# Attention with row sums on GpSimd: the last add of a group becomes a fifth adding transfer, and three orders of issue move

## What is computed

```python
attn = jnp.einsum('bhqd,bhkd->bhqk', q, k) * scale      # 16 heads of 32
attn = jax.nn.softmax(attn, axis=-1)
out = jnp.einsum('bhqk,bhkd->bhqd', attn, v)
```

## Time and profile before

| | |
|---|---|
| median of three runs | 4841.78 us (4838.85 to 4843.54) |
| the profiled execution's own time | 4836.55 us |
| its span, first to last instruction | 4834.7 us |
| PE busy | 4691.4 us, 97% of the span |
| POOL busy | 3223.0 us, 67% |
| DVE busy | 3170.4 us, 66% |
| ACT busy | 2398.9 us, 50% |
| adding transfers (L840) | 256, 1024 KB each, median 7.3 us from issue to landing |

### The profile page before, as it was taken

One profiled execution on the slowest core, in us unless ns is written; L12 is line 12 of the kernel. 1 busy time (PEld: TensorE's weight loads), 2 busy tenths in 40 slices (PEclk: granted clock), 3 DMA queues, 4 the chain that ended last, 5 costly groups with the idle time before them and its releaser, 6 DMA issues. The chain is left out here.

```text
span 4834.7 us, 66456 instructions
## 1 busy us (share of the span) xinstructions
PE 4691.4 (97%) x24396; PEld 2773.0 (57%) x24396; DVE 3170.4 (66%) x5296; ACT 2398.9 (50%) x4653; POOL 3223.0 (67%) x1117
## 2 busy tenths in 40 slices
PE   8999999999899999999999999999999999999979
PEld 6887878878654444444444444444444444444447
DVE  4223232333188888888888888888888888888534
ACT  2111121121146666666666666666666666666621
POOL 1121212121249998989989989999899998998920
PEclk9999999999979999999999999999999999999989
DMA  5344343343346655656656566665665656655466
GB/s 172 103 127 122 109 138 102 119 129 111 91 106 130 137 127 125 138 125 137 133 124 139 124 131 136 126 139 120 132 137 124 140 125 132 137 124 121 90 225 236
DMA packets 254215, 633.49 MB, mean 131 GB/s; under 512 B 45252, under 2 KB 79044, under 8 KB 212936
## 3 DMA queue, kind: packets, MB, share of 16 engines
q0 software_dynamic: 36864, 268.45, 27.8%
q1 hardware_dynamic: 217032, 360.85, 27.0%
HBM read 224.96 MB, written 134.74 MB: 74 GB/s over the span
## 5 line engine op out<-in xcount | busy, mean ns | idle before, releaser
L927 DVE TENSOR_REDUCE unit_max<-mx_ps 128x1 f32<-128x512 f32 x4096 | 2535.2, 681 | 317.0 <-PE mx_ps L1002 310.9
L836 POOL TENSOR_TENSOR p_pair<-p_sb 128x2048 f32<-128x2048 f32 x512 | 2439.8, 4811 | 185.3 <-PE mx_ps L1026 128.3
L913 ACT ACTIVATE p_sb<-st_ps 128x512 f32<-128x512 f32 x4096 | 2061.9, 628 | 905.5 <-PE st_ps L1073 905.5
L1002 PE MATMUL mx_ps<-k_x,q_x 96*128 96x512 f32 x4096 | 1684.9, 415 | 21.5 <-DMA k_x<-k_lo_d 19.6
L1073 PE MATMUL st_ps<-q_x,k_x 97*128 97x512 f32 x4096 | 1607.8, 413 | 37.9 <-ACT p_sb L913 37.3
L1073 PEld LDWEIGHTS st_ps<-q_x,k_x 97*128 97x128 f32 x4096 | 770.3, 188 | 599.3 <-ACT p_sb L913 512.8
L1002 PEld LDWEIGHTS mx_ps<-k_x,q_x 96*128 96x128 f32 x4096 | 784.6, 192 | 456.7 <-DVE unit_max L927 234.3
L1014 PE MATMUL o_ps<-p_sb,v_sb 128*32 128x512 f32 x8192 | 986.8, 599 | 0.0
L285 POOL TENSOR_TENSOR h_lo<-h_f,h_hi 128x512 fp32r<-128x512 f32 x128 | 165.2, 1291 | 687.7 <-DVE h_hi L469 687.7
L1014 PEld LDWEIGHTS o_ps<-p_sb,v_sb 128*32 128x32 f32 x8192 | 214.0, 109 | 494.1 <-ACT p_sb L913 309.8
L469 DVE CAST h_hi<-h_f 128x512 fp32r<-128x512 f32 x128 | 55.0, 431 | 541.9 <-ACT h_f L342 541.9
(11 more groups left out here) (94 smaller groups left out, 3926.8 us busy)
## 6 DMA issues: line engine op xcount, KB each, us to landing
p_pair<-p_pair POOLq DMA_DIRECT2D x256, 1024.0 KB, 7.3
q_x<-q_hi_d SPq DMA_DIRECT2D x128, 256.0 KB, 8.6
k_x<-k_hi_d SPq DMA_DIRECT2D x68, 256.0 KB, 7.3
xt<-x SPq DMA_DIRECT2D x64, 256.0 KB, 2.7
stage<-w SPq DMA_DIRECT2D x32, 512.0 KB, 5.1
q_hi_d<-qk_hi SPq DMA_DIRECT2D x64, 256.0 KB, 3.0
q_lo_d<-qk_lo SPq DMA_DIRECT2D x64, 256.0 KB, 3.9
k_hi_d<-qk_hi SPq DMA_DIRECT2D x64, 256.0 KB, 2.6
```

The costliest lines, as they stand in the source:

```text
L836: pool.tensor_tensor(p_pair[:, slot, :, :], p_sb[:, n % SLOTS, :, :], p_sb[:, (n + 1) % SLOTS, :, :], ALU.add).then_inc(pair_done, 1)
L913: act.activation(p_sb[:, (L * G * KT + n) % SLOTS, h, :], st_ps[bank(g, m)][:, :], ACT.Exp, scale=SCALE).then_inc(exp_done, 1)
L927: dve.reduce_max(unit_max[:, n // 4, n % 4:n % 4 + 1], mx_ps[UNIT_PLACE[n] % RING][:, :], AX.X).then_inc(bank_read, 1)
L1002: pe.matmul(mx_ps[UNIT_PLACE[n] % RING][:, :], q_x[qc][0:R, h, t * P:(t + 1) * P], k_x[u][0:R, h, kc * 512:(kc + 1) * 512], start=True, st ...
```

## The change

The ninth add of a group becomes a fifth `join` (so `NA` is 8 and `NJ` is 5), and the third sum waits for five joins. The next group's pair 0 goes ahead of the wait for it and pair 1 behind. `normalise` moves from behind the fourth join to ahead of pair 6. `spread_inverse` is split, and its store goes ahead of `load_shift`. In the strings, the unit behind the products moves to a later place of the step.

```diff
-    NA, NJ = NP + 1, 4
-    PARTS = [(2, 0, False, 7), (4, 0, True, 10), (0, NA, False, 11)]
+    NA, NJ = NP, 5
+    PARTS = [(2, 0, False, 7), (4, 0, True, 10), (5, 0, False, 11)]
...
-        STEPS = ["USUSUSUVUSSUSUSUS", "USUSUSUVUSSUSUSUS", "USUSUSUVZUSSUSUSUS", "USUSUSUVZUSSUSUSUS",
...
+        STEPS = ["USUSUSUVSSUSUUSUS", "USUSUSUVSSUSUUSUS", "USUSUSUVZSSUSUUSUS", "USUSUSUVZSSUSUUSUS",
...
-                def spread_inverse(count):
-
+                def store_inverse(count):
                     sp.wait_ge(inv_done, count)
                     sp.dma_start(inv_d.rearrange("h (r n) -> (h r) n", n=QR), inv_t[:, :]).then_inc(inv_st, 16)
+
+                def spread_inverse(count):
+
                     sp.wait_ge(inv_st, count * 16)
...
                             spread_sums(read_count(L, g, PART_PLACE[LAST_PART], first, last))
+                        if not (first and g == 0):
+                            store_inverse(L * G + g)
                         if not (last and g == G - 1):
                             load_shift(L * G + g + 2, (qc + 1) % QC)
...
                     if at > 0:
+                        pool.wait_ge(joined, (at * NJ - 1) * 16)
+                    pair(at, 0, a)
+                    if at > 0:
                         pool.wait_ge(joined, at * NJ * 16)
-                    pair(at, 0, a)
-                    pool.wait_ge(pair_done, at * NA)
                     pair(at, 1, b)
...
                     pair(at, 5, c)
+                    if at > 0:
+                        normalise(at)
                     pool.wait_ge(sum_done, at * NS + 1)
                     pair(at, 6, a)
                     pool.wait_ge(pair_done, at * NA + 6)
                     pool.wait_ge(joined, (at * NJ + 3) * 16)
                     join(d, c)
-                    if at > 0:
-                        normalise(at)
                     pair(at, 7, b)
                     pool.wait_ge(pair_done, at * NA + NP)
-                    pool.tensor_tensor(p_pair[:, a, :, :], p_pair[:, a, :, :], p_pair[:, b, :, :], ALU.add).then_inc(pair_done, 1)
+                    pool.wait_ge(joined, (at * NJ + 4) * 16)
+                    join(a, b)
```

More of the change, by code:

```diff
@@ L648, in attention_stage @@
         SK = 4 * KT
-        STEPS = ["USUSUSUVUSSUSUSUS", "USUSUSUVUSSUSUSUS", "USUSUSUVZUSSUSUSUS", "USUSUSUVZUSSUSUSUS",
-                 "USUSUSUVUSSUSUSUS", "USUSUSUVUSSUSUSUS", "USUSUSUVTUSSUSUSUS", "USUSUSUVZUSSUSUSUS"]
+        STEPS = ["USUSUSUVSSUSUUSUS", "USUSUSUVSSUSUUSUS", "USUSUSUVZSSUSUUSUS", "USUSUSUVZSSUSUUSUS",
+                 "USUSUSUVSSUSUUSUS", "USUSUSUVSSUSUUSUS", "USUSUSUVTSSUSUUSUS", "USUSUSUVZSSUSUUSUS"]
         FIRST = sum(s.count("U") for s in STEPS[AHEAD:])
@@ L807, in _ @@
                 spread_sums(ALL_READS + len(PARTS_AT) - PARTS_IN)
+                store_inverse(NQ * QC)
                 spread_inverse(NQ * QC)
```

## The result

The changed kernel takes 5035.9 us in the median of four runs (5024.07 to 5060.09), against 4842.66 us before (four runs as well): 1.0406 times as long, 95% interval 1.0366 to 1.0445. It is 193 us slower. Its profiled execution took 5038.24 us.

What follows compares the result with a forecast made beforehand. PE bounds the kernel now, but POOL's ring, 48.9 + 3.9 = 52.8 us, would set the period: +129 for 60 groups, -7 for the last four, +4 at the end, +126 on 4836.55, forecast 4968 us, range 4775 to 5040.

Steps and rivals of the forecast that it cites:

- POOL's ring: POOL's chain of joins and pairs through one group: 48.9 us base, 52.8 with slower landings, setting the period above PE's.
- The order on SP: Early product puts SP's loads ahead of join 4: lead 3.8 us, or 2.4 at a set's first group.
- named signs: Join 4 landing in 9 to 13 us, others 7.3; each set's first group longest; last four groups about 49.
- extra landing: Join 4's added landing time behind loads: 3.2 us ordinarily, 6.0 in a set's first group, mean 3.9 (3.0 to 5.3).
- the link from join 2 to join 3: Part of POOL's chain, a landing then an issue, with pair 4 hidden in it: 7.82 us.
- Work less lead: Join 4 ends behind the loads' work: for 1.5 MB, 7.0 us of work, lead 3.8, extra 3.2.
- It makes the product's new place possible: Inverses' store ahead of the shift row, load landing near 2534.6; costed at nothing by itself.
- The early product: Product ahead of pair 6, in POOL's 2.3 us wait for PE, ending ACT's wait: -0.87 us a group.
- the order of product and loads: Product ahead of pair 6 lets SP issue loads before join 4, lengthening its landing.
- The strings: PE's steps: three scores start one matmul earlier, ACT 0.23 us earlier; -0.8 us a group at best, 0 at worst.
- Landings that hardly grow: Rival: join 4 keeps 7.3 to 7.5 us, group 49.0 to 49.8, time 4744 to 4790, say 4765; chance 0.22.
- Half the extra: Rival: loads cost a transfer 1.2 to 2.9 us in the mean; 4808 to 4910 us, 4850 at 1.9; chance 0.12.

Runs made afterwards that it cites:

- experiment 8: The changed kernel without the loads for the next heads, so part of the work is left out: 4783.81 us, ratio 0.9878 to the kernel before.
- experiment 1: The changed kernel with the next heads' loads held until the fifth transfer of the group before has landed: 4854.55 us, ratio 1.0023 to the kernel before.
- experiment 7: The changed kernel with the loads held until pair 6 is done, to issue them together with the fourth transfer: 5102.65 us, ratio 1.0535.
- experiment 3: The kernel before with only the fifth transfer in place of the ninth add, the product staying behind the fourth transfer: 5046.16 us, ratio 1.0418.
- experiment 6: The changed kernel with its ninth add back on POOL and the loads held until the fourth transfer has landed: 4758.5 us, ratio 0.983.
- experiment 10: Early product, new strings, ninth add, loads held until the fourth landing, but the inverses' store back behind the shift row: 4883.11 us, ratio 1.0083.
- experiment 11: The kernel before with early product, early store of inverses, and loads held until the fourth transfer has landed: 4799.4 us, ratio 0.9911.
- experiments 5: The kernel before with only the early product and early store of the inverses, ninth add and old strings kept: 4977.46 us, ratio 1.0284.
- experiment 4: The kernel before with the new strings alone: 4813.94 us, ratio 0.9945.
- experiments 2: The changed kernel with its ninth add back on POOL and four transfers: 4944.65 us, ratio 1.0211 to the kernel before.

## Why the prediction was right, and where it was off

**The cause was right.** The forecast was 4968 us for 5035.9, slower. The range, 4775 to 5040, held it by only 4 us, and one of the four runs, at 5060, lies outside: that it held is in part luck. POOL's ring over the landings of the fourth and fifth transfers sets the period. Experiment 8 takes the loads away, and the ring falls to 49.5 us, near the base of 48.9 that the prediction had; experiment 1 moves them and gets 180 us back. The order on SP turned round with a lead of 3.8 us, as worked out from the product's place. At a set's first group it is 2.4 us, as forecast, though the prediction does not show how it gets from 3.5 us behind the last score to that lead. A set's first group is the longest, and the last four, without loads, are 48.9 to 51.2 us apart. Two of the named signs were a little off: at a set's first group join 4 lands in 14.1 us, not in 9 to 13, and join 2 in 7.8 us in the mean, not 7.3.

**The size was off by a third**: +126 us forecast, +193 measured. The mis-sized term is the ring's length, 52.8 us for 53.9, and 60 groups make that single microsecond some 60 us. Half of it is the fourth transfer's extra landing, 4.4 us in the mean (11.7 less 7.3) where I took 3.9: 3.6 for 3.2 in the ordinary groups and 6.8 for 6.0 in a set's first. The other half is the link from join 2 to join 3, 8.31 us for 7.82. I had read it from one group in the earlier trace rows that was on the short side (the mean before was 7.97), and the second transfer, too, now lands later. It does so without loads as well (7.7 us in experiment 8), and why is open. The range's upper end for the extra, 5.3, covered it.

**The rule behind the extra was only partly right.** "Work less lead" holds in experiment 1, where the loads are issued 4.9 us ahead of the first transfer, and 5.2 at a set's first group: it gives 9.4 and 12.6 us, and 9.4 and 12.6 were measured. In the changed kernel it gives 10.5 for 10.8 us at a lead of 3.8, and 15.4 for 14.1 at a set's first group. It fails at no lead (experiment 7), and it fails in experiment 3. There the loads are issued 5.3 us ahead of the fifth transfer, which makes 9.0 us for 1.5 MB, and 12.6 were measured. In the group shown the fourth transfer was on the way until 2731.84, over the first 4.8 us of that lead, so the lead on SP is not the lead in work; no run tests that by itself.

The Trainium skill (DMA: Bandwidth & Descriptors, "Queues, rings and completion order") has each DMA engine take turns between its queues, packet by packet. Even turns would make 12 us the ceiling, by an estimate: 7.3 us and the transfer's own work of 1 MB again, 4.7 us at the rate of the loads. The trace agrees in part: behind 1.5 and 1.75 MB the fourth transfer of the changed kernel keeps to it in the mean (10.8 and 11.2 us), behind 2.25 MB it does not (14.1), and in experiment 7 it keeps to it beside 1.5 MB alone. Whether the packets' unequal sizes or the ordered increment of the same section makes the difference, no run here tells.

**"It makes the product's new place possible", costed at nothing by itself.** With the loads held it is worth 125 us: the early product and the new strings gain 82 us with it (experiment 6) and lose 41 without it (experiment 10). In the changed kernel itself no run puts the store back.

**The early product was costed as a gain of 0.87 us a group.** With the loads held it is one (-43 us, experiment 11). As written it is worth +137 us, because it is what puts the loads ahead of the fourth transfer, and because it closes a second ring, through PE's sums and the inverses. I had the first half of this in the forecast, as a cause of the fifth transfer's trouble, and missed that it needs no fifth transfer. That it does need the loads is shown by the 180 us between experiments 5 and 11.

**A landing on the ring was looked for in one place.** The forecast named the order of product and loads as the cause. Experiment 3 keeps the old order and loses the same: the fifth transfer is then the one behind the loads. With five transfers in a group the loads have to meet one; the question is only which one has room. The forecast did not ask it.

**The strings** were costed at up to 0.8 us a group. A plain step went from 5.90 to 5.82 us in the changed kernel, and alone they gave 0.46 us a group (experiment 4). What they gave in the change itself no run shows. With the early product beside them they were worth 33 us (experiments 2 and 5), although PE did not set the period there.

**The rivals.** Landings that hardly grow would have given 4765 us: experiment 8, where they do not grow, takes 4784. Half the extra, at most 2.9 us, is out with 4.4 us measured. ACT's slots of `p_sb` were not a limit, as argued: no wait of ACT for a pair stands in the waits of the changed kernel.

## What to carry to other kernels

An add moved from an engine to a transfer frees the engine, but puts a landing where an add was: before doing it, add up the ring of waits through one period, landings included, and compare it with the bound engine's period, not the busy time. Then ask which transfer each bulk load is issued ahead of, and give the loads a place where the next transfer is far off. Here one wait on SP turned a change of +104 us into one of -82 us, and the fastest version kept the ninth add: there PE, not POOL, was the bound.

## What was not expected of the hardware

**A small transfer waits for large ones.** In experiment 1 the 8 KB load of the sums held DVE up for 4.18 us behind 2.25 MB. The loads of the inverses show the same. In the kernel before, no adding transfer was on the way when they were issued at 2536.32; in experiment 5 one was issued at 2740.83, in their midst. The DMA issues of the two, before first:

```profile
o_inv<-inv_d SPq DMA_DIRECT2D x4, 64.0 KB, 2.0
```

```profile
p_pair<-p_pair POOLq DMA_DIRECT2D x1, 1024.0 KB, 8.0
o_inv<-inv_d SPq DMA_DIRECT2D x4, 64.0 KB, 4.2
```

These are medians of the four: 2.0 us then and 4.2 us now. In experiment 5 the first two landed in 2.62 and 2.11 us and the last two in 5.86 and 6.65, and the early product waits for the last of them.

**PE's clock falls after a wait.** Stretches of the changed kernel around the wait at the second sum (columns as in the earlier trace rows):

```profile
2779.00:2782.00 3.00, 0.22 (x4) 0.19 (x8) 0.00 (x0) 0.00 (x0) 0.00 (x0) 1.00 0.44 90
2782.00:2783.50 1.50, 1.50 (x11) 0.64 (x4) 0.60 (x1) 0.19 (x1) 1.32 (x2) 0.99 0.00 0
2783.50:2786.70 3.20, 3.20 (x10) 2.43 (x9) 2.73 (x5) 2.26 (x5) 3.20 (x1) 0.50 1.01 205
2786.70:2790.00 3.30, 3.30 (x23) 1.56 (x25) 2.51 (x5) 1.94 (x4) 1.73 (x2) 0.97 0.59 119
```

PE did nothing but wait for nearly 3 us (0.22 us busy), went on at the full 2.4 GHz for 1.5 us, and then had a granted clock of 0.50, that is 1.2 GHz, for 3.2 us. There a matmul started every 0.43 us, and every 0.24 behind it. Over 2000 to 3000 us the mean clock is 0.98 where it was 1.00. Since the ring, not PE, set the period, it is not shown that this cost anything here.
